# A four-layer convolution and attention kernel: stacks of the first image on two queues, a first layer in column halves, and other PSUM rings

## The reference: what is computed

```
x = x + L0(gn(x))   # 3x3 Volterra convolution: 9 taps plus 45 products of two taps
x = x + L1(gn(x))   # 3x3 convolution (written as an FFT)
x = x + L2(gn(x))   # attention over pixels, then gates
x = x + L3(gn(x))   # Hartley transform, mix of 32x32 modes, transform back

# L2, cut to what is not zero (the hidden state is zero)
xin = W_in @ x + b_in
q = conv(xin, Wq, 'SAME')     # 4 heads of 8 channels, 1024 queries
k = conv(xin, Wk, 'VALID')    # 30x30 = 900 keys
v = conv(xin, Wv, 'VALID')
a = softmax(q^T k) v          # per image and head
gates = Wproj @ a + bias;  h = o * tanh(i * g);  out = W_out @ h + b_out
```

## Time and profile before

| | before |
|---|---|
| executions, us | 337.21, 338.34, 332.18 (median 337.21) |
| profiled execution, us | 337.82 |
| its span, us | 336.0 |
| PE busy | 296.6 us (88%) |
| DVE busy | 212.4 us (63%) |
| ACT busy | 176.7 us (53%) |
| POOL busy | 57.7 us (17%) |
| mean granted TensorE clock | 0.947 of full |

### The profile page before, as it was taken

How to read it: one execution, slowest core, us unless ns; L and a number is a source line. 1 busy time by engine, 2 the same in 40 slices (tenths; PEclk the granted TensorE clock), 3 DMA queues, 4 the chain that set the end, 5 groups by cost and what they waited for, 6 DMA issues and landing times. The chain is left out here.

```text
span 336.0 us, 10195 instructions
## 1 busy us (share of the span) xinstructions
PE 296.6 (88%) x4358; PEld 134.4 (40%) x4364; DVE 212.4 (63%) x476; ACT 176.7 (53%) x343; POOL 57.7 (17%) x84
## 2 busy tenths in 40 slices
PE   5899979798479995999999999999997999895893
PEld 2478523233244332333334344334342523344731
DVE  3991173555466365496888878888773214679935
ACT  1201101266345894698998989889897793100000
POOL 9500010289000000100101001010100108007000
PEclk9799999999755999699999999999999999997999
DMA  7100000016625899510000000000000000000001
GB/s 226 72 4 4 5 9 1 2 18 131 194 45 123 147 206 248 214 73 4 2 4 4 2 4 2 4 3 3 4 2 4 3 2 2 0 0 3 2 2 62
DMA packets 3844, 15.42 MB, mean 46 GB/s; under 512 B 1103, under 2 KB 1871, under 8 KB 3255
## 3 DMA queue, kind: packets, MB, share of 16 engines
q1 hardware_dynamic: 2823, 12.67, 15.2%
q0 software_dynamic: 976, 2.10, 2.1%
...
## 5 line engine op out<-in xcount | busy, mean ns | idle before, releaser
L786 ACT ACTIVATE arena_b<-ps 128x512 f32<-128x512 f32 x232 | 126.0, 616 | 27.6 <-PE ps L1323 25.4
L1296 PE MATMUL ps<-arena_a 72*32 72x450 bf16 x1024 | 95.3, 389 | 6.9 <-issue 4.7
L1323 PE MATMUL ps<-arena_a 75*32 75x512 bf16 x896 | 86.8, 386 | 4.7 <-DMA arena_a<-mt_sb 3.9
L988 DVE TENSOR_REDUCE mx<-ps 128x1 f32<-128x450 f32 x120 | 68.5, 616 | 4.8 <-PE ps L1296 4.8
L983 DVE CUSTOM_DVE_ANT_0 sums<-ps,relus 128x450 bf16<-128x450 f32 x68 | 42.2, 626 | 43.8 <-PE ps L1296 38.3
L1343 PE MATMUL ps<-arena_b,vt 128*32 128x512 f32 x448 | 58.1, 593 | 0.5 <-ACT arena_b L786 0.5
L1296 PEld LDWEIGHTS ps<-arena_a 72*32 72x32 bf16 x1024 | 29.4, 102 | 54.3 <-issue 20.8
L794 ACT ACTIVATE relus<-ps 128x450 f32<-128x450 f32 x68 | 38.0, 565 | 14.8 <-PE ps L1296 14.5
L1323 PEld LDWEIGHTS ps<-arena_a 75*32 75x32 bf16 x896 | 23.8, 96 | 45.0 <-ACT arena_b L786 20.1
L1164 PE MATMUL ps<-arena_a,cst 32*32 32x512 f32 x864 | 30.1, 627 | 1.7 <-ACT arena_a L717 1.7
L1134 PE MATMUL ps<-zeros 128*128 128x512 bf16 x80 | 20.7, 398 | 6.3 <-DMA xa<-x 3.5
...
...
## 6 DMA issues: line engine op xcount, KB each, us to landing
...
cst<-consts SPq DMA_DIRECT2D x1, 864.5 KB, 7.3
...
```

The source lines that it names most:

```text
L786: nc.scalar.activation(probs[:, n % PRING, :], ps[:, SCORE_RING[n % len(SCORE_RING)], :], ACT.Exp).then_inc(expd, 1)
L988: nc.vector.tensor_reduce(mx[:, a, e:e + 1], bank, AX.X, ALU.max).then_inc(max_read, 1)
L1296: last = mm(ps[32 * j:32 * j + 32, block_bank(i), 0:KHALF], qst[0:PAIR_ROWS, e, g, q0:q0 + 32], kst[0:PAIR_ROWS, g, at:at + KHALF], start= ...
L1323: last = mm(ps[32 * j:32 * j + 32, bank, :], kst[0:S_ROWS, g, k0:k0 + 32], qst[0:S_ROWS, e, g, :], start=True, stop=True)
```

## The change

**DMAs of the first image.** The twelve k DMAs of the first part are dealt out by head and part: six to SP (`SP_FIRST`), six to POOL (`POOL_FIRST`), each with its own semaphore. The second part of k is six on SP (heads 0 and 1) and six on POOL (heads 2 and 3). POOL's writes of k and of the first q half to DRAM come after these. SP's load of the second q half comes between the two heads' second parts.

```diff
-TOP = 18 * WP
-CUTS = ((0, TOP), (TOP, NP))
+
+CUTS = (slice(0, 18), slice(18, WP))
 COL_TILES = 4
+ALL = slice(0, 32)
...
+ADD_BEFORE = 7
...
-K_SECOND = slice(KEY0 + KHALF, KW)
+K_FIRST, K_SECOND = slice(0, KEY0 + KHALF), slice(KEY0 + KHALF, KW)
...
-MAX_RING = (3, 4, 5)
-O_RING = (6, 7)
+MAX_RING = (3, 4, 5, 7)
+O_RING = (6,)
...
+SP_FIRST = ((0, 0), (0, 2), (1, 1), (2, 0), (2, 2), (3, 1))
+POOL_FIRST = ((0, 1), (1, 0), (1, 2), (2, 1), (3, 0), (3, 2))
...
-            def stack_k_head(g, cols, signal):
-
-                for s in range(PARTS):
-                    sp.dma_start(kst[part_rows(s), g, cols], k_parts[HC * g:HC * (g + 1), :, cols]).then_inc(signal, 16)
+            def stack_k_head(g, s, cols, signal):
+
+                sp.dma_start(kst[part_rows(s), g, cols], k_parts[HC * g:HC * (g + 1), :, cols]).then_inc(signal, 16)
...
-            for g in range(HEADS):
-                stack_k_head(g, slice(0, K_SECOND.start), k_head[g])
-            sp.wait_ge(qd_written[1], PARTS * 16)
-            stack_q(1, 0, HEADS, q_second)
+            for g, s in SP_FIRST:
+                stack_k_head(g, s, K_FIRST, k_head[g])
 
             sp.wait_ge(k_padded, 1)
             sp.wait_ge(k_zeroed, 1)
             for s in range(PARTS):
                 sp.wait_ge(k_part[s], 3)
-            for g in range(HEADS):
-                stack_k_head(g, K_SECOND, k_second)
+            for s in range(PARTS):
+                stack_k_head(0, s, K_SECOND, k_second)
+            sp.wait_ge(qd_written[1], PARTS * 16)
+            stack_q(1, 0, HEADS, q_second)
+            for s in range(PARTS):
+                stack_k_head(1, s, K_SECOND, k_second)
             sp.wait_ge(m_in, 16)
...
-            sp.wait_ge(k_second, HEADS * PARTS * 16)
+                sp.wait_ge(k_head[g], in_list(SP_FIRST, g) * 16)
+                sp.wait_ge(k_head_pool[g], in_list(POOL_FIRST, g) * 16)
+            sp.wait_ge(k_second, 2 * PARTS * 16)
+            sp.wait_ge(k_second_pool, 2 * PARTS * 16)
```

```diff
             nc.gpsimd.memset(xp[:], 0.0).then_inc(xp_zeroed, 1)
-            nc.gpsimd.memset(vt[:], 0.0).then_inc(vt_zeroed, 1)
-            nc.gpsimd.memset(vrest[:], 0.0).then_inc(vt_zeroed, 1)
...
             rsqrt(0)
+            nc.gpsimd.memset(vt[:], 0.0).then_inc(vt_zeroed, 1)
+            nc.gpsimd.memset(vrest[:], 0.0).then_inc(vt_zeroed, 1)
...
-            pool.wait_ge(padded, 1)
+            pool.wait_ge(padded, 2)
...
-            image = interior(xp)
-            cols = on[:, 0, :].rearrange("p (y x) -> p y x", x=16)
-            n = 16
-            win_link(cols[:, :, 0:n], image[:, :, 0:n], image[:, :, n:2 * n], ALU.add)
...
+            def stack_k_part(g, s, cols, signal):
+
+                pool.dma_start(kst[s * PARTS * HC:(s + 1) * PARTS * HC, g, cols], k_parts[HC * g:HC * (g + 1), :, cols]
+                               ).then_inc(signal, 16)
...
             for s in range(PARTS):
-                pool.dma_start(q_dram[s, 0].rearrange("c g n -> g c n"), q_parts[:, s, 0:HALF]).then_inc(qd_written[0], 16)
+                pool.wait_ge(k_part[s], 2)
+            for g, s in POOL_FIRST:
+                stack_k_part(g, s, K_FIRST, k_head_pool[g])
             for s in range(PARTS):
                 pool.wait_ge(q_part[s], 2)
                 pool.dma_start(q_dram[s, 1].rearrange("c g n -> g c n"), q_parts[:, s, HALF:HW]).then_inc(qd_written[1], 16)
             for s in range(PARTS):
                 pool.wait_ge(k_part[s], 3)
+            for g in range(2, HEADS):
+                for s in range(PARTS):
+                    stack_k_part(g, s, K_SECOND, k_second_pool)
+            for s in range(PARTS):
                 pool.dma_start(k_dram[:, s].rearrange("c g n -> g c n"), k_parts[:, s, :]).then_inc(kd_written, 16)
+            for s in range(PARTS):
+                pool.dma_start(q_dram[s, 0].rearrange("c g n -> g c n"), q_parts[:, s, 0:HALF]).then_inc(qd_written[0], 16)
...
+                win_steps[0] += 1
...
+                win_link(cols[:, :, 0:n], image[:, :, 0:n], image[:, :, n:2 * n], ALU.add)
+                while n > 1:
```

```diff
+            for i, cut in enumerate(CUTS):
+                act.wait_ge(padded, i + 1)
+                nc.scalar.activation(columns(maps[:, 0, :], cut), columns(xp[:], cut), ACT.Copy).then_inc(act_map, 1)
+                nc.scalar.activation(columns(maps[:, 1, :], cut), columns(xp[:], cut), ACT.Square, scale=VOLTERRA_SCALE ** 0.5
...
-                return nc.vector.tensor_scalar(dst, src3(src, dst), mean, y, ALU.subtract, ALU.mult)
...
+                image = src.rearrange("p (y x) -> p y x", x=W)
+                for ys, xs in pieces:
+                    nc.vector.tensor_scalar(interior(xp)[:, ys, xs], image[:, ys, xs], mean, y, ALU.subtract, ALU.mult
+                                            ).then_inc(padded, 1)
+                return mean, y
...
-            norm_from_stats(xa[:], interior(xp)).then_inc(padded, 1)
...
+            norm_from_stats(xa[:], ((ALL, slice(0, 20)), (ALL, slice(20, W))))
+            dve.wait_ge(padded, 2)
...
-            nc.vector.scalar_tensor_tensor(xb[:], l0t, c_("l0bias"), xa[:], ALU.add, ALU.add).then_inc(l0_read, 1)
...
+                dve.wait_ge(first_loaded, 16)
+                dve.wait_ge(l0_summed, e + 1)
+                nc.vector.transpose(l0t[:, half].rearrange("p (j o) -> p j o", o=32),
+                                    ps[:, e, :].rearrange("p (i j) -> p j i", j=16)).then_inc(l0_read, 1)
+                dve.wait_ge(l0_read, 2 * e + 1)
+                nc.vector.scalar_tensor_tensor(xb[:, half], l0t[:, half], c_("l0bias"), xa[:, half], ALU.add, ALU.add
+                                               ).then_inc(l0_read, 1)
+                dve.wait_ge(l0_read, 2 * e + 2)
+                link(nc.vector.bn_stats(stats[:, 6 * e:6 * e + 6], xb[:, half]))
...
+            norm_from_stats(xb[:], ((slice(0, 14), ALL), (slice(14, H), ALL)))
...
+            norm_from_stats(xc[:], ((slice(0, 17), ALL), (slice(17, H), ALL)))
...
+                    dve.wait_ge(win_step, WIN_STEPS)
...
+            def add_taps(e):
...
+                    if e == 1 and i == ADD_BEFORE:
+                        pe.wait_ge(consts_loaded, 16)
+                        add_taps(0)
...
-                            last = mm(ps[32 * j:32 * j + 32, 2 * b + e, :].rearrange("p (y x) -> p y x", x=W),
-                                      l0w[r, COL_TILES * i + j, :], window(maps[r, m, :], py, px, 16 * e, 16, W),
+                            last = mm(ps[32 * j:32 * j + 32, 2 * b + e, :].rearrange("p (y x) -> p y x", x=16),
+                                      l0w[r, COL_TILES * i + j, :], half_window(maps[r, m, :], py, px, e),
...
-            for e in range(2):
...
+            add_taps(1)
```

135 lines of the change are left out of this document (66 added, 69 removed).

## The result

Twelve executions of the changed kernel took 331.33 us in the median (329.52 to 339.16), twelve of the kernel before 336.69 (332.18 to 341.35): a ratio of 0.987, 95% interval 0.983 to 0.991. In a second set it was 333.08 against 337.50, a ratio of 0.994 (0.989 to 0.999). The medians differ by 5.4 and 4.4 us, and the ratios amount to 4.4 and 2.0. So the change gives 2 to 5 us, where 10 were forecast. The time lies in the forecast's range, nearest to two of its rivals (331 and 332.6), but neither of them is what happened: that it lies there is in part luck, as the sum at the end shows.

What follows compares the result with a forecast made beforehand. PE, busy 88%, was taken as the bound, with time to gain only where it waits or runs slowly. Terms -1.0 - 0.75 - 0.8 - 0.75 - 7.6 + 0.5 = -10.4 from 337.8 gave 327.4, stated as 327.0 us (319.5 to 333).

Steps and rivals of the forecast that it cites:

- the start: Ahead of the first layer: memsets moved behind rsqrt and 20 columns normed first, PE begins near 9.0 us, -1.0 us.
- the first layer in column halves: First layer's matmuls read runs of 16 pixels, not 32: taken as 0, with +0.6 us if 2% slower.
- q's second half: Load on SP needed before the nine pairs behind the split: no wait taken, 0 (to +2 us).
- the rings: PSUM banks, four for maxima and one for outputs: 0 (-2 to +2 us), as PE was nearly full.
- the first image: First maxima: k DMAs on two queues end the 4.24 us wait for head 2; -7.6 us (-8.4 to -5.6).
- The rival of the DMA engines: DMA engines, not queues, limit the first image's heads, which come almost as late: 332.6 us, chance 0.13.
- The clock's 0.75: First layer: shorter gap ahead of it may keep the clock up; half of 1.5 us taken, -0.75 (0 to -1.5).
- The end of the first layer: Only half 1 remains to add, turn and measure: -1.85 us, against 1.07 for adding half 0 inside the layer; -0.8.
- Norms: Second and third norm written in two pieces, so consumers start 0.40 and 0.35 us earlier: -0.75 us.
- Behind the split: PE waits 2.8 us for the first split, the clock halves again, nine pairs take 10.1 us as before: 0 (to -3.9).
- Second maxima: PE's 3.88 us wait for the second maxima's DMA stays and grows as PE arrives earlier: +0.5 us (0 to +3.9).
- The rival in which it takes the gain back: PE reaches the second maxima earlier but their DMA lands no sooner, 3.9 us more wait: 331 us, chance 0.12.

Runs made afterwards that it cites:

- e3_queues: Kernel before with only the first image's stacking DMAs on two queues, their new order and later box sums; 329.2 us, ratio 0.982.
- e4_rings: Changed kernel with the PSUM rings of the kernel before (three banks for maxima, two for outputs); 331.5 us, ratio 0.990.
- e2_memsets: Changed kernel with POOL's memsets of vt and vrest behind both pieces of the first norm's write; 329.0 us, ratio 0.983.
- e10_fill: Changed kernel, memsets behind the first norm, mode weights in four pieces, 16 zero matmuls at first split, third norm's first piece 18 rows; 324.1 us, ratio 0.971.
- e1_after: The profile shown of the changed kernel, nothing else altered: one execution of 330.66 us with a span of 328.8.

## Why the prediction came out as it did

The steps that failed are three terms of the sum that promised too much: the start (-1.0, measured +1.0), the first layer in column halves (0 for the reading, measured +1.0, and +0.6 on the matmuls behind the adding), and q's second half (0, measured +1.84). One term promised too little: the rings (0, measured -2.4). The main term, the first image, held. One by one:

**What bounds the kernel, and the first image: right.** Heads were late by their issue. With two queues the wait for head 2 is gone, the pairs run at DVE's pace, and the stage gives 6.8 us (bounds -8.4 and -5.6), alone as well (e3_queues). The rival of the DMA engines is refuted: no head waits over 0.8 us.

**The start: wrong, and the step is named.** The prediction said that the memsets moved behind `rsqrt` "lie beside PE's 30 us of first layer". They did, but first they lay beside DVE's write, of which nothing was said. +1.03 us and not -1.0; with the memsets one step later it is -0.9 (9.13), as the sum had it. The clock's 0.75 was put down to the gap ahead of the layer, which was to shrink to 0.75 us; it was 1.73 and 2.89 in the two profiles of after, and the clock fell in both (in e4_rings, with the same start, it did not). In the eight profiles with the memsets moved it never fell at the layer's start, in six with the old start twice. The step cost 2 us, and some more through the clock, 3.4 and 6.8 us at half clock in the two profiles.

**The end of the first layer, and columns: wrong by 1.8.** From the layer's last matmul to the second layer's start it is 9.26 us by rows (e3_queues) and 7.30 by columns (e2_memsets); of these 1.96 us, 0.30 are the norm's, 1.66 the shorter end's (-1.85 forecast). The adding costs 1.0 as forecast. But columns cost 1.0 (0 taken, 0.6 as the bound), and the rounds behind the adding 0.6 more.

**Norms: one right, one wrong.** The second gave 0.30 (-0.40 forecast), the third nothing (PE waited 1.36 us for it, 1.34 before), for its odd number of rows.

**Behind the split: inside its bound.** q's second half was late by 1.84 us in both profiles of after and by 0 to 1.5 in the others; the forecast took 0, with +2 as the bound. Its place in SP's order was priced and not its landing: the three DMAs were issued by 88.88 us (86.16 + 2.72), 6 us before PE needed them, and PE could go on at 96.80; from 87.00 to 94.70 us the DMA engines were busy for 0.81 of the time. That the clock would fall there was right; that it hangs on the length of the wait was not: it fell behind 0.78 us too (e10_fill), and did not fall behind gaps of 1.48 and 1.34 us at the second and third norm of the kernel before.

**Second maxima: right in kind.** The wait stayed (2.78 and 3.26 us) and did not grow: -0.6 to -1.1 against the 3.88 of the sum's base, not +0.5; the second profile of before has 2.20, so no change is shown. The rival in which it takes the gain back is refuted.

**Rings: the term was mis-sized.** 0 was taken (-2 to +2). From the third turn to the eighth it is -2.4 us (103.97 before, 101.58 in e1_after), and -2.5 with the rings alone (101.44). The other 1.0 of the stage's 3.4 lies ahead of the third turn, where the clock was at 0.50 for 5.3 us before and for 3.4 after. The step read PE's 20.61 of 20.80 us as full. A busy PE in this profile includes matmuls whose modelled ends reach over stalls of 0.2 us; the weight loads' waits, which the prediction did not read, had 8.4 us for DVE's reductions in three half-images. At the boundary shown the values start 0.05 us behind the turn's end, as forecast; what the one output bank costs by itself was not run (the weight loads wait 1.2 us for it in three half-images).

**The base.** The sum was set against an execution of 337.82; the median of the 67 in the experiments is 336.4.

Together, from one profile to the other, against the sum of -10.4: start +2.0, first layer with norm and clock +2.6, third norm +0.35, first image +0.8, behind the split +2.4, second maxima -1.7, rings and the rest of the attention -3.4. That leaves -7.2, which is what the two profiled executions differ by. So 8.2 us were missed and 5.1 came back from terms put at 0 and +0.5: the errors cancelled in part. The first turn came 5.1 us earlier than 99.74, and not 10.5 (the sum's own terms ahead of it are 3.3 and 7.6, so 10.9). As to the device time, the medians differ by 4.4 to 5.4; that the rest lies in the clock of the executions is argued and not shown, since single profiles do not resolve it.
